# Adding the four components of a quaternion read by two VectorE sums instead of sixteen TensorE products

## The chip, the cores and the metric

One core of a Trainium2 chip runs the whole program once. The metric is the device time in microseconds (us); several executions are timed and their median is compared. Another execution is profiled; its span runs from its first to its last instruction. Below, PE is TensorE, DVE VectorE, ACT ScalarE, POOL GpSimd and SP the queue that issues DMAs.

## The reference, cut to what matters

Four layers follow each other on x of 4 x 1024 x 128: a time-mixing layer, a top-1 expert layer, a quaternion memory layer and a top-4 expert layer. The change is in the third:

```python
keys   = unit quaternions of (xn @ Wk.T + bk)       # 32 quaternions of 4 channels
values = (xn @ Wv.T + bv)
bound  = quat_mul(values, keys)
memory = jnp.cumsum(bound, axis=1)                  # over the tokens of a sequence
retrieved = quat_mul(memory, quat_conj(keys))       # the read
retrieved = retrieved / sqrt(position)
x = x + (layernorm(retrieved) * ln_g + ln_b) @ Wo.T + bo
```

Each output channel of a `quat_mul` is a sum of four products of a component of one factor with a signed component of the other.

## The kernel before, in words

All 4096 tokens stay in SBUF as `x_tok`. The memory layer is `memory_and_top4`. It takes 8 tiles of 512 tokens, each in 4 groups `s` of 128 tokens (a token per partition, 128 channels in the free dimension). The function `weave` writes out by hand what each engine issues: for tile `i` a `body` of 16 steps, and in each step first `tail(i-1)`, then `main(i)`, `ahead(i+1)` and `norm(i+2)`. So four tiles are under way, and each engine takes its instructions in this order. Behind the 8 bodies come `units`, the top-4 expert layer, 17 units a tile; the tail of tile 7 runs in its first ones, and its routing for tile 0 (`route`, `look`) runs in the bodies of tiles 6 and 7.

What a body does, by step, with the lines that the text speaks of:

- `ahead`: PE makes keys (`c_k`, L1453 and L1455, step 0) and values (`c_v`, step 4). ACT copies the keys in four signed orders (`key`, L1854 and L1860). DVE makes 1/length (L1625 a `tensor_reduce` over 4 adjacent elements, L1628, L1631) and divides the values by it (L1636, L1638).
- `main` step 0: products of key and value into `bound`, [128, s, 4 components, 128]: DVE s = 0 and 1 (L1647), POOL s = 2 and 3 (L1973).
- steps 1, 3, 5, 7: PE adds the four components and sums over the tokens in one go, with the triangular matrix `upto` as the moving operand (L1478), and adds the sum carried from the group before (L1483); ACT copies each result to `memory` (L1873).
- steps 8, 9: DVE divides `memory` by the key's length (L1653, and L1658 for s = 2 and 3 as `memory_n`).
- step 10: products for the read, into `read`: DVE s = 0, 1 (L1664), POOL s = 2, 3 (L1979).
- step 12: DVE makes the real part `real` (L1670, one for s = 0, 1 and one for s = 2, 3).
- steps 12 to 15: PE adds the four components of each group with the identity (L1494), sixteen products a tile, into the bank `bank_r`.
- `tail` steps 0 to 4: DVE makes `got` = 2 real - sum (L1678), its mean and variance (L1683, L1689), and, after POOL's power (L1985, L1989), the shift (L1693). Steps 6, 7: ACT normalises (L1881). Step 8: PE transposes (L1505), ACT L1888; step 11: PE multiplies with Wo (`c_o`); step 13: DVE adds the residual (L1698), which POOL had put ready at step 4 of `main` (`kept`, L1966).
- `norm`: statistics of the tile two ahead (DVE L1606, L1613, L1618; POOL L1957), ACT `xn` (L1839), and at step 12 PE transposes it (L1449) and ACT copies it (`xt`, L1846).

The lines around the change that a sentence can't say:

```python
for m in range(QC):                                     # L1493, PE, QC = 4
    mm = pe.matmul(bank_r[:, s * P:(s + 1) * P], ident, read[:, s, m, :], start=(m == 0), stop=(m == QC - 1))
...
dve.wait_ge(read_out, i + 1)                            # L1676, DVE, in front of got
```

An fp32 product of this shape leaves two records in the trace, so the 128 products of L1494 stand there as 256.

Of the kernel before, what the change touches and what calls it, by code (L numbers as in the profile page):

```python
# [9 lines left out]
ALU = mybir.AluOpType  # L10
ACT = mybir.ActivationFunctionType
AXIS = mybir.AxisListType
# [6 lines left out]
P = 128  # L19
BATCH, SEQ = 4, 1024  # L20
TOKENS = BATCH * SEQ
SUB = 4
# [52 lines left out]
def need(engine, semaphore, value):  # L75

    if not isinstance(value, int) or value > 0:
        engine.wait_ge(semaphore, value)
# [1026 lines left out]
QUATS, QC = P // 4, 4  # L1105
# [93 lines left out]
def memory_and_top4(nc, x_tok, consts, weights, out_dram, moe):  # L1199
# [3 lines left out]
    with ExitStack() as ctx:  # L1203
# [6 lines left out]
        def sem(name):  # L1210
            return nc.alloc_semaphore("c_" + name)
# [4 lines left out]
        ident = consts[:, C_AT["ident"][0]:C_AT["ident"][1]]  # L1216
# [47 lines left out]
        bound_dve, bound_pool = sem("bound_dve"), sem("bound_pool")  # L1264
        memory_out, memory_ready, memoryn_ready = sem("memory_out"), sem("memory_ready"), sem("memoryn_ready")
        read_dve, read_pool = sem("read_dve"), sem("read_pool")
        read_out, real_ready, got_ready = sem("read_out"), sem("real_ready"), sem("got_ready")
        stats2_ready, moments2_ready, var2_ready = sem("stats2_ready"), sem("moments2_ready"), sem("var2_ready")
        rstd2_ready, shift2_ready, normed_ready = sem("rstd2_ready"), sem("shift2_ready"), sem("normed_ready")
        normedt_out, normedt_ready, wo_out, x_ready = sem("normedt_out"), sem("normedt_ready"), sem("wo_out"), sem("x_ready")  # L1270
# [133 lines left out]
        with nc.Block() as block:  # L1404
# [38 lines left out]
            def _(pe):  # L1443
# [24 lines left out]
                def main(i, h, step):  # L1468
                    if step in (1, 3, 5, 7):
                        s = step // 2  # L1470
                        if s < 2:
                            pe.wait_ge(bound_dve, 2 * i + s + 1)
                        else:
                            pe.wait_ge(bound_pool, 2 * i + s - 1)
                        need(pe, memory_ready, SUB * i + s - 1)
                        carried = h or s
                        for m in range(QC):
                            mm = pe.matmul(bank_m[s % 2][:, 0:P], w("upto"), bound[:, s, m, :],  # L1478
                                           start=(m == 0), stop=(m == QC - 1 and not carried))
                        if carried:  # L1480
                            pe.wait_ge(memory_ready, SUB * i + s)
                            before = memory[:, h, s - 1, :] if s else memory[:, 1 - h, SUB - 1, :]
                            mm = pe.matmul(bank_m[s % 2][:, 0:P], w("last"), before, start=False, stop=True)  # L1483
                        mm.then_inc(memory_out, 1)
                    if step >= 12:
                        s = step - 12
                        if s == 0:
                            need(pe, got_ready, i)
                        if s < 2:
                            pe.wait_ge(read_dve, 2 * i + s + 1)  # L1490
                        else:
                            pe.wait_ge(read_pool, 2 * i + s - 1)
                        for m in range(QC):  # L1493
                            mm = pe.matmul(bank_r[:, s * P:(s + 1) * P], ident, read[:, s, m, :],  # L1494
                                           start=(m == 0), stop=(m == QC - 1))
                        if s == SUB - 1:
                            mm.then_inc(read_out, 1)

                def tail(i, h, step):
                    if step == 8:  # L1500
# [100 lines left out]
            def _(dve):  # L1601
# [39 lines left out]
                def main(i, h, step):  # L1641
                    if step == 0:
                        dve.wait_ge(valuen_ready, 2 * (i + 1))
                        dve.wait_ge(key_ready, i + 1)
                        need(dve, memory_out, SUB * i)
                        for s in (0, 1):
                            dve.tensor_tensor(in_quats(bound[:, s, :, :]), in_quats(key[:, h, s, :, :]),  # L1647
                                              spread_component(early_value[:, s, :]), ALU.mult).then_inc(bound_dve, 1)
                    if step == 8:
                        dve.wait_ge(memory_ready, SUB * (i + 1) - 2)  # L1650
                        dve.wait_ge(valuen_ready, min(2 * i + 3, 2 * TILES) if isinstance(i, int) else 2 * i + 3)
                        need(dve, real_ready, 2 * i)
                        dve.tensor_tensor(by_quat(early_n), by_quat(memory[:, h, 0:2, :]), per_quat(rnorm[:, h, 0:2 * QUATS]),  # L1653
                                          ALU.mult).then_inc(memoryn_ready, 1)
                    if step == 9:
                        dve.wait_ge(memory_ready, SUB * (i + 1))
                        need(dve, read_pool, 2 * i)
                        dve.tensor_tensor(by_quat(memory_n[:, :, :]), by_quat(memory[:, h, 2:4, :]), per_quat(rnorm[:, h, 2 * QUATS:]),  # L1658
                                          ALU.mult).then_inc(memoryn_ready, 1)
                    if step == 10:  # L1660
                        dve.wait_ge(memoryn_ready, 2 * (i + 1))
                        need(dve, read_out, i)
                        for s in (0, 1):
                            dve.tensor_tensor(in_quats(read[:, s, :, :]), in_quats(key[:, h, s, :, :]),  # L1664
                                              spread_component(early_n[:, s, :]), ALU.mult).then_inc(read_dve, 1)
                    if step == 12:
                        need(dve, got_ready, i)
                        for first, part in ((0, early_n), (2, memory_n[:, :, :])):
                            k0 = key[:, h, first:first + 2, 0, 0:P:QC]
                            dve.tensor_tensor(components(real[:, first:first + 2, :]), components(part),  # L1670
                                              k0.unsqueeze(3).broadcast_to([P, 2, QUATS, QC]), ALU.mult).then_inc(real_ready, 1)

                def tail(i, h, step):
                    if step == 0:
                        dve.wait_ge(real_ready, 2 * (i + 1))
                        dve.wait_ge(read_out, i + 1)  # L1676
                        need(dve, normed_ready, i)
                        dve.scalar_tensor_tensor(got[:, :, :].rearrange("p s c -> p (s c)"), real[:, :, :].rearrange("p s c -> p (s c)"),  # L1678
                                                 2.0, bank_r[:, :], ALU.mult, ALU.subtract).then_inc(got_ready, 1)
                    if step == 1:  # L1680
                        dve.wait_ge(got_ready, i + 1)
                        for s in range(SUB):
# [267 lines left out]
            def _(pool):  # L1950
# [11 lines left out]
                def main(i, h, step):  # L1962
# [11 lines left out]
                                               spread_component(value_n[:, s - 2, :]), ALU.mult).then_inc(bound_pool, 1)  # L1974
                    if step == 10:
                        pool.wait_ge(memoryn_ready, 2 * (i + 1))
                        need(pool, read_out, i)
                        for s in (2, 3):
                            pool.tensor_tensor(in_quats(read[:, s, :, :]), in_quats(key[:, h, s, :, :]),  # L1979
                                               spread_component(memory_n[:, s - 2, :]), ALU.mult).then_inc(read_pool, 1)  # L1980
# [134 lines left out]
```

## Time and profile before

| what | us |
|---|---|
| median of 3 runs | 950.02 (945.75 to 951.28) |
| the profiled execution, its own time | 945.13 |
| its span | 943.3 |
| its memory layer, first `got` to last | 491.4 to 598.9 |
| mean granted TensorE clock | 0.905 of 2.4 GHz |

A row of a timeline gives the start in us from the span's start, the duration in us, the engine, the line, the operation, what it writes and reads, and in brackets how long the engine had been idle before it and which instruction ended that. "x8" means eight merged instructions, whose duration is then that from the first start to the last end. "issue" is idle time that the view could give to no other engine.

### The profile page before, as it was taken

What the parts mean: (1) busy time and instruction counts of PE and PEld (TensorE: products, weight loads), DVE (VectorE), ACT (ScalarE), POOL (GpSimd) and SP (SyncE); (2) the same over time, 40 slices, a digit from 0 to 9 for tenths busy, and PEclk for the clock granted to TensorE, in tenths of its full rate; (3) what the DMA queues carried; (4) which work ended last, traced back from release to release, by engine and by line L of the source; (5) the groups of instructions that cost most, each with busy time, mean ns of one, the idle gap of its engine ahead of it and who ended that gap; (6) DMA issues with size and microseconds to landing.
All of it is one profiled execution on the core that took longest, in us unless ns stands there. A gap on an engine that the chain in (4) does not pass through costs nothing.

```text
span 943.3 us, 14234 instructions
## 1 busy us (share of the span) xinstructions
PE 789.7 (84%) x3827; PEld 563.7 (60%) x3828; DVE 653.4 (69%) x1483; ACT 429.4 (46%) x861; POOL 465.2 (49%) x424
## 2 busy tenths in 40 slices
PE   5888888996495599992289999899999999999997
PEld 2344444442395366661278888668686776868685
DVE  3899999998474133336458777686877868686864
ACT  3344445541121132233246555466565656657453
POOL 3465556664047133336136555355565555555564
PEclk9999999997555699996579999999999999999999
DMA  5000000000394111112000000537191745638090
GB/s 170 0 1 2 0 1 0 0 1 0 52 384 151 35 48 48 45 42 101 0 1 1 2 1 1 114 68 161 36 190 39 155 86 109 131 63 176 20 189 12
DMA packets 35662, 62.15 MB, mean 66 GB/s; under 512 B 3360, under 2 KB 15136, under 8 KB 34832
## 3 DMA queue, kind: packets, MB, share of 16 engines
q1 hardware_dynamic: 33328, 56.75, 25.5%
q0 software_dynamic: 2272, 4.67, 1.5%
q8 instruction: 27, 0.44, 0.2%
q14 instruction: 35, 0.29, 0.1%
HBM read 53.13 MB, written 8.28 MB: 65 GB/s over the span
## 4 chain that ended last, share of the span: by engine, by line
PE 24%; issue 11%; POOL 10%; DVE 3%; ACT 2%; DMA 1%; POOLq 0%; SPq 0%; ACTq 0%; DVEq 0%
POOL d_hid_lo L2006 5%; PE c_m L1513 2%; PE c_m L1515 2%; PE c_m L1514 2%; PE c_o L1564 1%; PE c_r L1564 1%; PE c_k L1513 1%; POOL c_bound L1973 1%; POOL c_read L1979 1%; PE c_k L1514 1%; PE c_k L1515 1%; PE c_v L1513 1%; PE c_o L1562 1%; PE c_o L1561 1%; PE c_v L1515 1%
## 5 line engine op out<-in xcount | busy, mean ns | idle before, releaser
L2006 POOL TENSOR_TENSOR d_hid_lo<-c_bound,d_hid_hi 128x512 fp32r<-128x512 f32 x136 | 176.1, 1295 | 156.1 <-ACT d_hid_hi L1936 155.8
L580 POOL TENSOR_TENSOR a_rs<-a_r,a_state 128x512 f32<-128x512 f32 x64 | 75.4, 1184 | 79.8 <-DVE a_state L432 74.1
L1936 ACT ACTIVATE d_hid_hi<-c_bound 128x512 fp32r<-128x512 f32 x136 | 85.2, 626 | 46.2 <-DVE c_bound L1804 45.6
L432 DVE TENSOR_TENSOR_SCAN a_state<-a_decay,a_state,a_vb 128x512 f32<-128x512 f32 x64 | 81.4, 1272 | 0.0
L1016 DVE TENSOR_TENSOR b_hidden<-b_h,b_b 128x512 f32<-128x512 f32 x39 | 27.0, 692 | 78.0 <-PE b_h L836 78.0
L1098 POOL DMA_INDIRECT results<-b_y_row,b_result_row x39 | 37.1, 953 | 86.3 <-DVE b_y_row L1022 86.3
L1795 DVE TENSOR_TENSOR c_m<-c_bound,c_m 128x512 f32<-128x512 f32 x64 | 44.2, 691 | 26.5 <-PE c_m L1515 20.5
L1795 DVE TENSOR_TENSOR c_v<-c_bound,c_v 128x512 f32<-128x512 f32 x64 | 44.2, 691 | 23.9 <-PE c_v L1515 18.7
L1513 PE MATMUL c_m<-d_x_hi,d_hi 128*128 128x512 f32 x136 | 55.8, 411 | 1.9 <-DVE c_bound L1804 1.9
L850 PEld LDWEIGHTS b_y<-b_w,b_hidden_t 128*128 128x128 f32 x312 | 39.1, 194 | 25.3 <-issue 25.2
L1515 PE MATMUL c_m<-d_x_hi,d_lo 128*128 128x512 f32 x136 | 53.9, 396 | 0.0
L1514 PE MATMUL c_m<-d_x_lo,d_hi 128*128 128x512 f32 x136 | 53.8, 395 | 0.0
L836 PE MATMUL b_h<-b_w,b_xin_t 128*128 x78 | 45.6, 668 | 7.1 <-issue 5.8
L1926 ACT ACTIVATE c_bound<-c_k 128x512 f32<-128x512 f32 x60 | 35.7, 595 | 34.4 <-PE c_k L1515 33.9
L1926 ACT ACTIVATE c_bound<-c_m 128x512 f32<-128x512 f32 x60 | 35.7, 595 | 34.3 <-PE c_m L1515 33.9
L570 POOL TENSOR_TENSOR a_xf<-a_lerp,a_xt 128x512 f32<-128x512 f32 x40 | 43.3, 1091 | 10.3 <-DVE a_lerp L395 10.0
L416 DVE TENSOR_TENSOR a_vb<-a_k,a_vb 128x512 f32<-128x512 f32 x64 | 43.2, 687 | 3.8 <-PE a_vb L304 3.8
L303 PE MATMUL a_vb<-a_v_hi,a_spread 128*128 128x512 f32 x64 | 44.5, 695 | 1.1 <-DVE a_state L432 1.1
L850 PE MATMUL b_y<-b_w,b_hidden_t 128*128 x312 | 44.3, 286 | 0.8 <-ACT b_hidden_t L1078 0.8
L1092 POOL DMA_INDIRECT rows_in<-b_rows,b_index x32 | 30.9, 965 | 26.7 <-DVE b_index L956 17.6
L1804 DVE TENSOR_TENSOR c_bound<-c_v,d_w_wide 128x512 f32<-128x512 f32 x56 | 38.7, 691 | 6.9 <-DMA d_w_wide<-pair_weights 4.5
L1075 ACT ACTIVATE b_xin_t<-b_x 128x128 f32<-128x128 f32 x38 | 10.6, 278 | 68.6 <-PE b_x L831 68.6
(299 smaller groups left out, 2184.0 us busy)
## 6 DMA issues: line engine op xcount, KB each, us to landing
d_w_wide<-pair_weights SPq DMA_DIRECT2D x64, 512.0 KB, 11.8
b_w<-in_w SPq DMA_DIRECT2D x2, 2048.0 KB, 15.5
d_raw<-in_moe SPq DMA_DIRECT2D x3, 1088.0 KB, 30.6
b_xin<-rows_in SPq DMA_DIRECT2D x39, 64.5 KB, 1.8
b_b<-in_b SPq DMA_DIRECT2D x1, 2048.0 KB, 21.9
b_rows<-results SPq DMA_DIRECT2D x4, 512.0 KB, 5.1
out<-c_read SPq DMA_DIRECT2D x8, 256.0 KB, 2.5
a_weights<-in_mixing SPq DMA_DIRECT2D x1, 901.0 KB, 6.5
```

The source lines that it names most:

```text
L303: pe.matmul(vb[n][:, :], row, v_hi[:, h, :], start=True, stop=False)
L432: dve.tensor_tensor_scan(state[:, j, seq_cols(h, 1)], decay[:, h, :], vb[j % 3][:, :], first, ALU.mult, ALU.add).then_inc(scan_ready, 1)
L580: pool.tensor_tensor(rs[:, j, :], rr[:, h, :], state[:, j, seq_cols(h, 0)], ALU.mult).then_inc(rs_ready, 1)
L836: pe.matmul(bank_h[h][:, :], xin_t[:, h, :], w1[:, bass.ds(e * D_FF, D_FF)], start=True, stop=True).then_inc(h_out, 1)
L850: mm = pe.matmul(bank_y[h][:, 0:P], hidden_t[:, h, f * P:(f + 1) * P], w2[:, bass.ds(e * D_FF + f * P, P)], start=(f == 0), stop=(f == FF_ ...
L1513: pe.matmul(out, weights_hi, moving_hi, start=start, stop=False)
L1514: pe.matmul(out, weights_hi, moving_lo, start=False, stop=False)
L1515: return pe.matmul(out, weights_lo, moving_hi, start=False, stop=stop)
L1795: dve.tensor_tensor(bank_3[r][:, :], silu[:, r, :], bank_3[r][:, :], ALU.mult).then_inc(product_ready, 1)
L1926: act.activation(silu[:, r, :], bank_1[r][:, :], ACT.Silu).then_inc(silu_ready, 1)
L1936: act.activation(hid_hi[:, r, :], hidden[:, r, :], ACT.Copy).then_inc(hi_ready, 1)
L2006: pool.tensor_tensor(hid_lo[:, r, :], hidden[:, r, :], hid_hi[:, r, :].bitcast(F32), ALU.subtract).then_inc(lo_ready, 1)
```

## The change

PE's sixteen products with the identity, and PE's waits around them, go. DVE gets two `tensor_reduce` instructions a tile, at steps 13 and 15 of `main`, each over two groups: 1024 elements in, 256 out, the summed axis being the components, which lie 128 elements (512 bytes) apart. `got` then reads both its operands from SBUF, where it read one from PSUM. The semaphore `read_out` (PE) is replaced by `summed` (DVE).

```diff
@@ PE, main
-                    if step >= 12:
-                        s = step - 12
-                        if s == 0:
-                            need(pe, got_ready, i)
-                        if s < 2:
-                            pe.wait_ge(read_dve, 2 * i + s + 1)
-                        else:
-                            pe.wait_ge(read_pool, 2 * i + s - 1)
-                        for m in range(QC):
-                            mm = pe.matmul(bank_r[:, s * P:(s + 1) * P], ident, read[:, s, m, :],
-                                           start=(m == 0), stop=(m == QC - 1))
-                        if s == SUB - 1:
-                            mm.then_inc(read_out, 1)
@@ DVE, main
                     if step == 10:
                         dve.wait_ge(memoryn_ready, 2 * (i + 1))
-                        need(dve, read_out, i)
...
+                    if step in (13, 15):
+                        if step == 13:
+                            dve.wait_ge(read_dve, 2 * (i + 1))
+                            need(dve, normed_ready, i)
+                        else:
+                            dve.wait_ge(read_pool, 2 * (i + 1))
+                        pair = slice(0, 2) if step == 13 else slice(2, 4)
+                        dve.tensor_reduce(got[:, pair, :], read[:, pair, :, :].rearrange("p s m c -> p s c m"), AXIS.X,
+                                          ALU.add).then_inc(summed, 1)
@@ DVE, tail
                     if step == 0:
                         dve.wait_ge(real_ready, 2 * (i + 1))
-                        dve.wait_ge(read_out, i + 1)
-                        need(dve, normed_ready, i)
-                        dve.scalar_tensor_tensor(got[:, :, :].rearrange("p s c -> p (s c)"), real[:, :, :].rearrange("p s c -> p (s c)"),
-                                                 2.0, bank_r[:, :], ALU.mult, ALU.subtract).then_inc(got_ready, 1)
+                        dve.wait_ge(summed, 2 * (i + 1))
+                        dve.scalar_tensor_tensor(got[:, :, :], real[:, :, :], 2.0, got[:, :, :],
+                                                 ALU.mult, ALU.subtract).then_inc(got_ready, 1)
@@ POOL, main
                     if step == 10:
                         pool.wait_ge(memoryn_ready, 2 * (i + 1))
-                        need(pool, read_out, i)
+                        need(pool, summed, 2 * i)
```

## Rows read from the trace of the kernel before

**Rows 1.** Stretches `got` to `got`: length, busy PE PEld DVE ACT POOL (count), clock, DMA

```profile
521.24:536.17 14.93, 13.94 (x108) 12.42 (x108) 11.89 (x33) 8.53 (x23) 8.81 (x9) 1.00 0.00 0
536.17:553.05 16.88, 15.62 (x106) 13.91 (x106) 12.02 (x33) 8.52 (x23) 8.81 (x9) 0.90 0.01 1
...
567.98:582.47 14.49, 13.34 (x104) 11.95 (x105) 11.68 (x33) 7.82 (x22) 8.82 (x9) 1.00 0.01 2
```

**Rows 2.** Timeline of DVE, the body between two `got`

```profile
521.24 0.69 DVE L1678 SCALAR_TENSOR_TENSOR c_got<-c_real,c_r 128x512 f32<-128x512 f32 x1 [1.88 <-issue]
...
530.39 0.42 DVE L1658 TENSOR_TENSOR c_memory_n<-c_memory,c_rnorm 128x256 f32<-128x256 f32 x1
...
532.38 1.30 DVE L1670 TENSOR_TENSOR c_real<-c_memory_n,c_key 128x256 f32<-128x256 f32 x1
533.61 0.68 DVE L1698 TENSOR_TENSOR x_tok<-c_o,c_kept 128x512 f32<-128x512 f32 x1
536.17 0.69 DVE L1678 SCALAR_TENSOR_TENSOR c_got<-c_real,c_r 128x512 f32<-128x512 f32 x1 [1.89 <-issue]
```

**Rows 3.** Timeline of PE, the same body

```profile
522.59 1.16 PE L1478 MATMUL c_m<-c_bound,memory_weights 128*128 128x128 f32 x8
...
528.44 0.39 PE L1483 MATMUL c_m<-c_memory,memory_weights 128*128 128x128 f32 x2
...
532.80 0.60 PE L1449 MATMUL c_x<-shape_consts,c_xn 128*128 128x128 f32 x4
533.23 2.84 PE L1494 MATMUL c_r<-c_read,shape_consts 128*128 128x128 f32 x24
...
536.44 1.16 PE L1455 MATMUL c_k<-memory_weights,c_xt 128*128 128x128 f32 x8
```

**Rows 4.** Timelines of ACT and POOL, the same body

```profile
529.34 0.27 ACT L1873 ACTIVATE c_memory<-c_m 128x128 f32<-128x128 f32 x1
...
530.51 1.65 ACT L1839 ACTIVATE c_xn<-x_tok,c_shift,c_rstd 128x128 f32<-128x128 f32 x4
533.43 0.60 ACT L1846 ACTIVATE c_xt<-c_x 128x512 f32<-128x512 f32 x1 [1.27 <-PE c_x L1449]
```

```profile
533.36 2.68 POOL L1973 TENSOR_TENSOR c_bound<-c_key,c_value_n 128x512 f32<-128x512 f32 x2
```

**Rows 5.** Groups of instructions by form: count, busy us, mean ns of one, idle before

```profile
L1494 PE MATMUL c_r<-c_read,shape_consts 128*128 128x128 f32 x256 | 32.1, 280 | 2.1 <-DVE c_read L1664 2.1
```

```profile
L1625 DVE TENSOR_REDUCE c_norm<-c_square 128x128 f32<-128x512 f32 x8 | 5.3, 666 | 14.1 <-ACT c_square L1856 13.9 <-issue 0.2
```

**Rows 6.** Lines L960 (reads 32 bytes apart), L946 (adjacent): duration ns min/median/max

```profile
L960 DVE TENSOR_REDUCE b_here<-b_chosen x8: 171/206/208, 264.1 to 294.4; 128x8 f32<-128x32 f32 x8
```

```profile
L946 DVE TENSOR_REDUCE b_position<-b_own_place x8: 180/180/186, 268.3 to 296.9; 128x4 f32<-128x32 f32 x8
```

**Rows 7.** Timeline of PE: gaps, and the instructions behind them

```profile
58.05 1.82 PE L244 MATMUL a_front<-a_xa,a_weights 128*128 128x512 f32 x2 [2.58 <-DVE a_xa L387]
...
487.00 1.16 PE L1494 MATMUL c_r<-c_read,shape_consts 128*128 128x128 f32 x8 [1.55 <-DVE c_read L1664]
...
547.78 1.92 PE L1494 MATMUL c_r<-c_read,shape_consts 128*128 128x128 f32 x8
...
608.03 0.80 PE L1513 MATMUL c_v<-d_x_hi,d_hi 128*128 128x512 f32 x1 [2.93 <-DVE c_bound L1804]
```

**Rows 8.** Busy time by stretch behind three gaps of PE, columns as in rows 1

```profile
58.00:61.00 3.00, 2.95 (x5) 1.64 (x6) 3.00 (x7) 0.60 (x1) 0.53 (x2) 0.56 0.00 0
...
111.00:114.00 3.00, 2.45 (x6) 1.06 (x6) 3.00 (x8) 0.79 (x2) 0.56 (x2) 1.00 0.00 0
```

```profile
608.00:611.40 3.40, 3.37 (x11) 2.75 (x11) 3.37 (x12) 2.29 (x4) 1.77 (x2) 0.51 1.07 210
```

**Rows 9.** Timeline of DVE, the last body and the first unit

```profile
587.60 0.29 DVE L1737 TENSOR_REDUCE d_minus_max<-c_d 128x4 f32<-128x128 f32 x1 [0.82 <-PE c_d L1515]
...
607.28 0.69 DVE L1804 TENSOR_TENSOR c_bound<-c_v,d_w_wide 128x512 f32<-128x512 f32 x1 [4.45 <-DMA d_w_wide<-pair_weights]
```

More of the change, by code:

```diff
@@ L1266, in memory_and_top4 @@
         read_dve, read_pool = sem("read_dve"), sem("read_pool")
-        read_out, real_ready, got_ready = sem("read_out"), sem("real_ready"), sem("got_ready")
+        summed, real_ready, got_ready = sem("summed"), sem("real_ready"), sem("got_ready")
         stats2_ready, moments2_ready, var2_ready = sem("stats2_ready"), sem("moments2_ready"), sem("var2_ready")
```

## The prediction, on record before the changed kernel ran

> **What bounds the kernel now.** I read the stretches from one `got` (L1678) to the next first, since each is one tile of the memory layer. There are seven. Four last 14.92 to 14.94 us, of which one is shown; one 16.88, the only one at a mean clock below full; then 14.49, and a last one that holds the first routing [rows 1]. In the shown stretch PE is busy 13.94 us and DVE 12.42: two engines close to the length, so the timeline has to say which waits for which. DVE waits 1.88 or 1.89 us in front of `got` [rows 2]. The view calls it issue, but PE's last products of L1494 end at 533.23 + 2.84 = 536.07 and `got` starts at 536.17 [rows 2, 3]: DVE waits for the work that the change removes. Behind `got` comes DVE's half of `bound`, and PE's next c_m waits for that (it starts at 522.59, 1.35 after `got` at 521.24) [rows 2, 3]. So the loop is closed through both engines. But between the two waits for `got` DVE has almost nothing free: from 521.24 to the end of L1698 at 533.61 + 0.68 = 534.29 is 13.05 us, with one larger wait in it, for POOL's power.
>
> **What goes.** L1494 holds PE 32.1 us in 8 tiles, 4.0 a tile [rows 5]. What the time gets back is not that but DVE's wait, at most 1.89 us a tile, because DVE's 13.05 us stay. PE's waits at these steps go too. The waits of DVE and POOL at step 10 are met by DVE's order (the sums of a tile stand long before its successor's reads), and the wait for `normed` moves to step 13, long after ACT has normalised. No DMA moves.
>
> **What comes.** Two sums of 1024 elements. The nearest row is L1625: 512 elements in 0.666 us; L946 takes 0.180 for 32 [rows 5, 6]. The slope is 0.486 / 480 = 1.01 ns an element, so 1024 take 0.666 + 0.52 = 1.18 us. Neighbouring DVE instructions overlap by 0.08 (533.61 starts before 532.38 + 1.30 = 533.68 [rows 2]), so each adds 1.10. The low bound is 1.05, a nanosecond an element with nothing fixed left. The high bound comes from the distance between summed elements. L1625's are adjacent, the new ones 512 bytes apart. L960 sums elements 32 bytes apart: 206 ns in the median, but 171 in its shortest, against 180 at L946 with adjacent ones [rows 6]. Taken at its worst that is 26 / 32 = 0.81 ns more an element, 0.83 us more a sum, 2.0 us each. I take 1.18, because the shortest of the strided ones shows no penalty at all, and the others start right on the heels of a tiny conversion, whose end their record may include.
>
> The Trainium skill speaks against this change here: "Advanced Engine Details and Errata", section SBUF Cachelines, says that accesses that each hit another 16-byte line pay a penalty. By that rule the sums would be dear, and the rival below says how dear; the 171 ns speak against it, the 206 for it.
>
> `got` now reads two operands from SBUF. What that can cost is shown by L1670's second instruction: 1.30 us for 256 elements while POOL's multiplications of the read ran, and it ended 0.32 behind POOL's switch from L1979 to L1973 at 533.36 [rows 2, 4]. It had waited for POOL. POOL's `bound` products end at 533.36 + 2.68 = 536.04 [rows 4]. The new `got` comes after that (next paragraph), so I take nothing; at worst it starts when POOL ends, which costs nothing either while the sums end later.
>
> **The sum, a tile at full clock.** The first sum starts at 534.21, the second ends at 534.21 + 2 x 1.10 + 0.08 = 536.49, `got` starts 0.04 later, at 536.53. Before it was 536.17 [rows 2]. So a tile loses 0.36 us: 2.24 of sums against 1.89 of wait. Over the bodies: four with 14.93 give +1.44. The one of 16.88 becomes 15.29, -1.59, since its length came from PE running at half clock, which DVE would no longer wait for. The one of 14.49 has a larger wait and comes out at +0.05. The one before the first `got` is a draw. Tile 7's sums and `got` run about 1 us later, and are covered by the 4.45 us in which DVE waits for the weights of the first unit [rows 9]. Together -0.1 us: at full clock the change is worth nothing.
>
> **PE's clock.** PE now gets a hole. Its transposes of `xn` can start when ACT is done at 530.51 + 1.65 = 532.16 [rows 4] and end 0.6 later; ACT's copy takes 0.60 and the keys 1.53 (from 536.07 to 536.44 + 1.16), until about 535.0 [rows 3, 4]. The next c_m can start only 1.35 behind `got`, at 537.88. That is a hole of over 2.8 us a tile where PE was without one. What such holes do here is in the trace. In the time-mixing layer PE waits some 2.6 us (2.58 at 58.05) or more in front of L244 in each of seven tiles; behind six of these waits the clock fell to 1.2 GHz, as at 58 to 61 (mean 0.56), and behind one, at 111 to 114, it stayed at 2.4 [rows 7, 8]. After 2.93 us at 608.03 it fell too (0.51) [rows 7, 8]. After 1.55 us at 487.00 it stayed [rows 7]. At half clock eight records of L1494 take 1.92 us and not 1.16 [rows 7].
>
> What it costs: the low stretch at 608.0 to 611.4 lasts 3.4 us [rows 8], in which PE does half the work and falls 1.7 us behind. The c_m ends at 528.44 + 0.39 = 528.83; ACT's copy of it starts at 529.34 and ends 529.61, and DVE wants it at 530.39 [rows 2, 3, 4]. The slack is 0.44 + 0.78 = 1.2 us. So one stretch costs 0.5 us; two in a row, where the first begins inside the hole, 3.4 - 1.2 = 2.2. I take 0.9, nearer to the single one. And not every tile pays: a PE that is late also has a shorter hole the next time. I take four of the six tiles, +3.6. Then the last body. Body 6 has no keys to make, so the hole there is from 10.9 + 0.6 behind `got` to 14.5 + 1.35, some 4.4 us. Behind it stand c_m and the logits, and DVE already waits 0.82 for those at L1737 [rows 9], the chain that leads over the weights and their DMA to 607.28. No slack: +1.7. (To +3.4 with two.)
>
> **The sum.** -0.1 + 3.6 + 1.7 = +5.2 us. The profiled execution took 945.13 by its own time (span 943.3); the median of the runs is 950.02, 4.9 above it, so I put the difference on the median: 955.2.
>
> **Rivals.**
> - *The clock stays up* (or its loss falls into slack). For it: one of seven holes passed without a fall, DVE is the bound, and PE then has 4 us to spare. Against: the other six. Time: 950.02 - 0.1 = 949.9, no change that can be measured. It decides at a hole below about 2 us.
> - *The strided sums cost 2.0 us each*, the rule of "Advanced Engine Details and Errata" as a mechanism of this kernel: DVE as the plain bound, 17 us a tile. 7 bodies x 2 x 0.83 = 11.6 more on top: 966.8. Against it the 171 ns.
> - *Not slower, faster*: PE sets the pace of the loop and DVE has hidden room, so that removing PE's work lets DVE's chain close up, where it waits for POOL's power and where L1670 waits for POOL. If the order of POOL and DVE shifts so that L1670 runs before POOL's products (0.42 in place of 1.30 [rows 2]), a tile gains 0.9 - 0.36 = 0.5 us, in 7 bodies 3.8, and the slow stretch of 16.88 stays away: about 945. It decides if L1670's second instruction falls below 1 us. Against: both wait for the same `memory_n`, and DVE's reads stand first.
> - *The edit does something else than it says*, say the sum is split into more instructions: not visible in the diff, covered by the second rival.
>
> **How the numbers follow.** About 0.5%, 4.75 us, is what a measurement of this kernel can tell from no change. Forecast case, time lost through the clock: 0.54, its own range 951 to 961. Clock stays up: 0.22. Dear strides: 0.12. Faster: 0.08. The rest, 0.04, beyond all. The range of 8 in 10 runs from 946 (the clock stays up, with the spread of 5 us between runs of before) to 966, near dear strides. Slower by over 0.5% (above 954.8): 0.32 of the forecast case, dear strides 0.12, and the rest 0.04: 0.48. Within: the forecast case's lower 0.22 and the 0.22 in which the clock stays up: 0.44. Faster: 0.08.
>
> **What would show it.** No L1494 on PE; sixteen `tensor_reduce` of 1024 elements on DVE at 1.15 to 1.25 us (2.0 under the stride rival); `got` to `got` 15.3 us where the clock is full; `got` with no idle time before it; holes of 2 to 3 us in front of c_m (L1478), and mean clocks of 0.8 to 0.9 in the stretches behind; DVE idle in front of L1658 in those, which it isn't now; in the last body L1737 waiting over 2 us. DVE's busy time rises by 2.2 a tile, 18 us. I am wrong if the stretches sit at 15.3 with full clock everywhere (then no change), if they are under 14.9 (then DVE had room that I didn't see), or over 16.5 at full clock (then the sums are dear).

## The result, and the profile after

| what | before | after |
|---|---|---|
| median of 4 runs, us | 950.65 (945.75 to 952.4) | 973.24 (972.16 to 974.08) |
| ratio | | 1.026 [1.023, 1.0291] |
| profiled execution, its own time | 945.13 | 972.16 |
| its span | 943.3 | 970.3 |
| mean granted clock | 0.905 | 0.881 |

The kernel became slower: the ratio on record is 1.026 (the quotient of the two medians is 1.024), 22.6 us in the medians and 27.0 in the profiled executions. The forecast was 955.2, the range ended at 966. The lines of the changed kernel are numbered anew: `got` L1672, the sums L1665, `bound` L1634, `memory_n` L1645, the read L1650, shift L1687.

The stretches from one `got` to the next, columns as in [rows 1]:

```profile
494.97:513.03 18.06, 12.78 (x75) 10.86 (x75) 15.79 (x36) 8.36 (x23) 8.80 (x9) 0.84 0.00 0
513.03:530.39 17.36, 12.08 (x73) 10.23 (x73) 15.65 (x36) 8.36 (x23) 8.81 (x9) 0.90 0.01 1
530.39:547.83 17.44, 12.16 (x75) 10.31 (x75) 15.64 (x35) 8.36 (x23) 8.81 (x9) 0.90 0.00 0
547.83:566.40 18.57, 13.29 (x73) 11.15 (x73) 15.64 (x36) 8.36 (x23) 8.81 (x9) 0.79 0.01 1
...
601.85:622.45 20.60, 16.55 (x100) 14.43 (x101) 17.07 (x52) 10.13 (x24) 6.15 (x7) 0.72 0.02 6
```

The reader sees three things. DVE's busy time rose from 12.0 to 15.7 us a tile (3.7, where the forecast had 2.2). No stretch has the full clock any more. And in the first six the length exceeds DVE's busy time by 1.7 to 2.9 us, where 1.3 are left at full clock (filled_hole, below), so DVE is not all of it. The group of the sums gives their price; its shortest, 1866 ns, is nearly as dear as its median:

```profile
L1665 DVE TENSOR_REDUCE c_got<-c_read x16: 1866/1918/1991, 491.1 to 620.4; 128x256 f32<-128x1024 f32 x16
```

DVE and PE in the third stretch:

```profile
530.39 0.69 DVE L1672 SCALAR_TENSOR_TENSOR c_got<-c_real,c_got 128x512 f32<-128x512 f32 x1
531.00 1.28 DVE L1634 TENSOR_TENSOR c_bound<-c_key,c_v 128x512 f32<-128x512 f32 x2
...
534.98 1.22 DVE L1687 SCALAR_TENSOR_TENSOR c_shift<-c_moments,c_rstd 128x4 f32<-128x4 f32 x1 [0.83 <-POOL c_rstd L1983]
...
540.17 0.42 DVE L1645 TENSOR_TENSOR c_memory_n<-c_memory,c_rnorm 128x256 f32<-128x256 f32 x1 [0.55 <-ACT c_memory L1867]
...
542.17 1.29 DVE L1656 TENSOR_TENSOR c_real<-c_memory_n,c_key 128x256 f32<-128x256 f32 x1
543.38 0.68 DVE L1692 TENSOR_TENSOR x_tok<-c_o,c_kept 128x512 f32<-128x512 f32 x1
543.99 3.74 DVE L1665 TENSOR_REDUCE c_got<-c_read 128x256 f32<-128x1024 f32 x2
547.83 0.69 DVE L1672 SCALAR_TENSOR_TENSOR c_got<-c_real,c_got 128x512 f32<-128x512 f32 x1
```

```profile
531.73 2.08 PE L1478 MATMUL c_m<-c_bound,memory_weights 128*128 128x128 f32 x8 [3.71 <-DVE c_bound L1634]
...
544.30 1.16 PE L1455 MATMUL c_k<-memory_weights,c_xt 128*128 128x128 f32 x8
549.17 2.07 PE L1478 MATMUL c_m<-c_bound,memory_weights 128*128 128x128 f32 x8 [3.71 <-DVE c_bound L1634]
```

`got` has no idle time before it, where it had 1.89 [rows 2]; the sums take its place and 1.9 us more. PE, which had no hole there, waits 3.71 us, and the first c_m behind the hole takes 2.08 and not 1.16 [rows 3]: the clock has fallen. DVE then waits 0.55 for ACT's copy of that late product, a wait that was absent in the stretch shown of before; in the six bodies between the first `got` and the seventh it is 0.46 to 1.68.

**Where the 27.0 us are**, from start times in the two timelines:

| part | before | after | more |
|---|---|---|---|
| to the stage's first PE instruction (L1449) | 461.07 | 463.19 | 2.1 |
| from there to the first `got` | 30.3 | 31.8 | 1.5 |
| first `got` to last | 107.5 | 127.5 | 20.0 |
| last `got` to the first product with `w_wide` | 8.4 | 5.9 | -2.5 |
| from there to the first copy of `y` | 46.9 | 48.9 | 2.0 |
| the seven tiles of units behind it | 283.2 | 286.9 | 3.6 |
| the end | 5.8 | 6.1 | 0.3 |

The first line is not the change's: in twelve other profiled executions it ranges from 457.5 to 464.2, with no relation to the edit. Below, "the stage" is the second to fourth line together: 146.2 us before, 165.1 after. The 146.2 hold the one body of 16.88 us [rows 1], 2 us longer than its neighbours.

### The profile page after: what moved, and what is told of

Same layout as the page of the kernel before. It is cut to its first block, busy times and chain, and to the rows that moved or that the text cites. A ratio compares the mean times of both kernels' runs of the same rounds, so it can differ in the third digit from the quotient of the medians.

```text
span 970.3 us, 13731 instructions
## 1 busy us (share of the span) xinstructions
PE 781.1 (80%) x3571; PEld 549.6 (57%) x3572; DVE 685.9 (71%) x1499; ACT 427.8 (44%) x861; POOL 462.9 (48%) x424
## 4 chain that ended last, share of the span: by engine, by line
PE 27%; issue 9%; DVE 8%; POOL 6%; ACT 3%; POOLq 0%; DVEq 0%; ACTq 0%
POOL d_hid_lo L2000 5%; PE c_m L1478 4%; DVE c_got L1665 3%; PE c_m L1500 2%; PE c_m L1502 2%; PE c_m L1501 2%; PE c_o L1551 1%; PE c_r L1551 1%; PE c_k L1500 1%; PE c_k L1501 1%; PE c_k L1502 1%; PE c_o L1549 1%; PE c_o L1548 1%; PE c_v L1502 1%; PE c_v L1500 1%
## 5 line engine op out<-in xcount | busy, mean ns | idle before, releaser
L1478 PE MATMUL c_m<-c_bound,memory_weights 128*128 128x128 f32 x256 | 46.9, 347 | 27.2 <-DVE c_bound L1634 27.2
L1478 PEld LDWEIGHTS c_m<-c_bound,memory_weights 128*128 128x128 f32 x256 | 43.3, 257 | 28.7 <-DVE c_bound L1634 28.7
## 6 DMA issues: line engine op xcount, KB each, us to landing
d_w_wide<-pair_weights SPq DMA_DIRECT2D x64, 512.0 KB, 11.6
```

## The experiments

Theories for the 19 us of the stage: **S**, the sums cost 1.92 us and not 1.18, and DVE is the bound; **C**, the clock falls in PE's hole; **O**, the new body brings DVE's and POOL's instructions together in a worse order. Each run is timed against the kernel before on its own chip. The table has what all of them gave. The columns are the ratio of the times as it stands on record, with its 95% interval (it can differ by 0.2% from the quotient of the medians), then, from one profiled execution each, the stage, a typical body (the middle ones), and the clock in it.

| run | ratio | stage | body | clock |
|---|---|---|---|---|
| before | 1 | 146.2 | 14.93 | 1.00 |
| after_again | 1.0253 [1.0216, 1.0291] | 165.1 | 17.4 to 18.5 | 0.79 to 0.90 |
| adjacent | 1.0213 [1.0175, 1.025] | 159.1 | 16.9 to 17.2 | 0.80 |
| filled_hole | 1.0259 [1.0217, 1.0301] | 165.2 | 16.9 | 1.00 |
| drop_only | 0.9905 [0.9868, 0.9943] | 136.5 | 13.4 to 14.0 | 0.88 to 1.00 |
| add_only | 1.0173 [1.0135, 1.0212] | 158.4 | 16.65 | 1.00 |
| layout | 1.0218 [1.0181, 1.0255] | 159.1 | 16.8 to 17.2 | 0.80 |
| ordered_strided | 1.0183 [1.0153, 1.0213] | 159.7 | 16.8 to 17.5 | 0.84 to 0.90 |
| ordered_layout | 1.0133 [1.0106, 1.016] | 155.7 | 15.6 to 16.9 | 0.80 to 0.89 |
| ordered_layout_filled | 1.0157 [1.0141, 1.0172] | 159.4 | 15.3 to 15.6 | 1.00 |
| before_ordered | 0.9993 [0.998, 1.0005] | 144.7 | 14.6 to 14.8 | 1.00 |
| hybrid_plain | 0.9988 [0.9974, 1.0002] | 141.2 | 14.4 | 1.00 |
| hybrid | 0.9915 [0.9899, 0.993] | 139.6 | 13.5 | 1.00 |

**adjacent: the same number of elements, summed over four neighbours.** The output is made of other numbers.

```diff
-dve.tensor_reduce(got[:, pair, :], read[:, pair, :, :].rearrange("p s m c -> p s c m"), AXIS.X,
+dve.tensor_reduce(got[:, pair, :], read[:, pair, :, :].rearrange("p s m (q c) -> p s (m q) c", c=QC), AXIS.X,
```

> The changed kernel, but each sum runs over four adjacent channels of one component in place of the four components 512 bytes apart (same element counts, so the output is other numbers). If the distance between summed elements makes the sums dear: 1.18 us each where the changed kernel has 1.92, got to got 15.3 to 16 us, and a time of 958 to 964, 10 or more below the changed kernel. If size or shape (1024 in, 256 out) or POOL beside it makes them dear: still 1.9 us and 973. If the clock alone makes the loss: sums may shorten, but the time stays above 968.

The group of the sums in this run, then its PE and a DVE instruction in one body:

```profile
L1665 DVE TENSOR_REDUCE c_got<-c_read x16: 1201/1202/1208, 484.9 to 608.2; 128x256 f32<-128x1024 f32 x16
```

```profile
521.73 2.08 PE L1478 MATMUL c_m<-c_bound,memory_weights 128*128 128x128 f32 x8 [2.31 <-DVE c_bound L1634]
523.61 0.63 PE L1483 MATMUL c_m<-c_memory,memory_weights 128*128 128x128 f32 x2
524.03 1.91 PE L1478 MATMUL c_m<-c_bound,memory_weights 128*128 128x128 f32 x8
...
531.39 0.42 DVE L1645 TENSOR_TENSOR c_memory_n<-c_memory,c_rnorm 128x256 f32<-128x256 f32 x1 [1.74 <-ACT c_memory L1867]
```

The stride costs 1918 - 1202 = 716 ns a sum, 0.70 ns an element. But this run is also the forecast's own world, sums at 1.2 us, and it is still 2.1% slower than before. Behind a hole of 2.3 us the clock is down for two groups of c_m, in every body but the first, and DVE then waits 1.5 to 1.8 us for the late product. These bodies take 16.9 to 17.2 us with DVE busy for 14.2. So the sums' price came as the first theory had it, and its body of 15.3 to 16 us did not.

**filled_hole: after, with sixteen products with the identity behind the keys, which nobody reads.**

```diff
 project(bank_k, "bk", "wk", xt).then_inc(k_out, 1)
+for s in range(SUB):
+    for m in range(QC):
+        pe.matmul(bank_r[:, s * P:(s + 1) * P], ident, w("upto"), start=(m == 0), stop=(m == QC - 1))
```

> The changed kernel with sixteen products of the identity put behind the keys on PE, into a bank that nobody reads, so that PE's hole is filled with as much work as was taken out. If the fallen clock costs what the waits in front of L1645 (7.5 us) and L1731 (2.4) and the first unit show: full clock in the memory layer, got to got 17.0 in every body, 962 to 966. If the sums alone make the loss: 971 to 973, no change.

Its stretches:

```profile
529.18:546.05 16.87, 14.29 (x110) 12.39 (x109) 15.62 (x35) 8.53 (x23) 8.82 (x9) 1.00 0.00 1
546.05:562.93 16.88, 14.14 (x108) 12.24 (x107) 15.63 (x35) 8.53 (x23) 8.81 (x9) 1.00 0.01 1
```

With PE filled the clock stays at 2.4 GHz in six bodies (mean 0.99 in the sixth). The middle four take 16.87 to 16.90 us, near the 17.0 of the first theory, and before's timeline says why: the sums begin 534.21 - 521.24 = 12.97 behind `got` as the forecast had it, and take 3.84 until the next `got` (543.99 to 547.83 above), together 16.81. So at full clock S alone is the whole body. C is 127.5 - 122.1 = 5.4 us from first to last `got`. The time gained nothing that the ratio shows (1.0259), because the same products run at half clock where the stage starts and nothing covers them; the first `got` comes 37.4 us behind the stage's first instruction, not 31.8. PE in that start, where the view puts the fillers under c_r:

```profile
460.24 2.07 PE L1455 MATMUL c_k<-memory_weights,c_xt 128*128 128x128 f32 x8
462.11 5.44 PE L1466 MATMUL c_r<-memory_weights,shape_consts 128*128 128x128 f32 x32
...
477.01 4.85 PE L1466 MATMUL c_r<-memory_weights,shape_consts 128*128 128x128 f32 x32
```

**drop_only and add_only: each half of the change alone.** The first leaves the sum of the components out altogether (`got` = 2 real - real). The second keeps PE's products and lets DVE also make the sums of tiles 0 to 6, into a buffer that nobody reads.

```diff
 # drop_only, against after
-dve.tensor_reduce(got[:, pair, :], read[:, pair, :, :].rearrange("p s m c -> p s c m"), AXIS.X,
-                  ALU.add).then_inc(summed, 1)
+dve.sem_inc(summed, 2)
-dve.scalar_tensor_tensor(got[:, :, :], real[:, :, :], 2.0, got[:, :, :],
+dve.scalar_tensor_tensor(got[:, :, :], real[:, :, :], 2.0, real[:, :, :],
```

> The removal alone: no products of L1494 and no sums (the sum is left out, got is made from real alone). DVE as the bound: got to got 13.2 to 14.9 at full clock (13.05 of DVE's own, and got, with two SBUF operands, may wait for POOL's products of bound until 14.8). With the clock falling as in the changed kernel one or two bodies of it are given back: 943 to 952. If PE had set the pace alone: got to got 11, 922.

> The addition alone: the kernel before, with the two strided sums of tiles 0 to 6 made on DVE beside PE's products and read by nobody. If the sums on DVE are the larger loss: got to got 17.0 (13.05 + 3.74 and the seam) at full clock, since PE has no hole: 950 + 7 x 2.1 = 964 or somewhat over. If the clock were the larger loss: the sums would still fill the 1.9 us of wait and little more, 955 to 958.

A body of each, drop_only first:

```profile
513.09:526.53 13.44, 10.74 (x77) 8.84 (x77) 12.29 (x35) 8.52 (x23) 9.27 (x10) 1.00 0.00 0
```

```profile
524.56:541.20 16.64, 14.02 (x107) 12.42 (x107) 15.49 (x36) 8.52 (x24) 8.83 (x9) 1.00 0.00 0
```

Even for nothing in return, PE's sixteen products are worth 1.5 us a body (less in the two of 13.98 and 13.93 us, in which the clock fell behind a hole of only 0.87) and 1% of the time: that is the ceiling of the change. The sums alone cost 1.7 us a body and 1.7%, at full clock, though PE's holes in front of c_m are 1.6 us in these bodies. In drop_only `got` starts while POOL still multiplies, and takes this:

```profile
513.09 1.16 DVE L1667 SCALAR_TENSOR_TENSOR c_got<-c_real 128x512 f32<-128x512 f32 x1
```

That is 1.16 and not the 0.69 of [rows 2]. In the changed kernel the sums push `got` behind POOL and it takes 0.69, as the forecast said.

**after_again and layout.** The first repeats the changed kernel beside the others. The second writes `read` with the four components adjacent, so that the sums are cheap and are still those of the components:

```diff
-read = sb("read", [P, SUB, QC, P])
+read = sb("read", [P, SUB, P, QC])
```

> The changed kernel once more, so that it stands on the same chip as the three below. Sums of 1.92 us, got to got 17.3 to 18.6, some 2.3 to 2.7% above the kernel before.

> The changed kernel with read laid out so that the four components of a channel are adjacent: the same sums and the reference's output, read by DVE at distance 4 bytes in place of 512; the products of DVE and POOL (L1650, L1973) now write elements 16 bytes apart. If distance between elements costs in reads alone: sums 1.20 us, products 0.68 and 1.27 as before, got to got 17.0 with the clock falling as in the run with adjacent sums, some 10 us under the changed kernel. If writes at a distance cost as much as reads: the products take 0.36 more each, DVE's four writes of 512 a tile give back 0.7 of the 1.4 saved, and POOL's take 1.6 us and are on the path to the second sum.

Who pays for the turned layout, DVE's read products, POOL's and the sums:

```profile
L1976 POOL TENSOR_TENSOR c_read<-c_key,c_memory_n 128x512 f32<-128x512 f32 x16 | 20.3, 1291 | 23.2 <-DVE c_memory_n L1648 23.2
L1668 DVE TENSOR_REDUCE c_got<-c_read 128x256 f32<-128x1024 f32 x16 | 18.6, 1204 | 0.0
L1653 DVE TENSOR_TENSOR c_read<-c_key,c_v 128x512 f32<-128x512 f32 x16 | 16.5, 1116 | 0.3
```

Beside them the same products of adjacent, which write as the kernel before does:

```profile
L1973 POOL TENSOR_TENSOR c_read<-c_key,c_memory_n 128x512 f32<-128x512 f32 x16 | 20.0, 1270 | 23.9 <-DVE c_memory_n L1645 23.9
L1650 DVE TENSOR_TENSOR c_read<-c_key,c_v 128x512 f32<-128x512 f32 x16 | 10.3, 683 | 0.3
```

Writes 16 bytes apart cost DVE 433 ns a product and POOL some 20. Yet layout and adjacent have the same stage, 159.1, and DVE is busy for the same 14.2 to 14.3 us a body. The reason is the second real part, which takes 0.63 us here and 1.29 in adjacent:

```profile
537.56 0.63 DVE L1659 TENSOR_TENSOR c_real<-c_memory_n,c_key 128x256 f32<-128x256 f32 x1
```

In both runs it ends 0.3 us behind POOL's read products (534.67 against 534.39 in adjacent, 538.19 against 537.92 here). So the dearer writes used time in which the real part would have been held up beside POOL. Against after_again layout is 0.35% lower and adjacent 0.40%, which the intervals don't separate from nothing; the stage is 6.0 us shorter in each.

**ordered_strided and ordered_layout: theory O.** POOL's `kept` waits for DVE's shift and POOL's `bound` for `got`; the second real part moves behind the sums. On the changed kernel, and on layout.

```diff
 # POOL, main, steps 4 and 0
+need(pool, shift2_ready, i)
+need(pool, got_ready, i)
 # DVE, main
     if step == 12:
         real_part(h, 0, early_n)
...
+    if step == 15:
+        real_part(h, 2, memory_n[:, :, :])
```

> The changed kernel, sums still 512 bytes apart, with three moves that keep DVE's instructions with two SBUF operands away from POOL's: kept (L1960) waits for the shift, POOL's products of bound wait for got, and the second real part comes behind the sums. If DVE sets the pace through waits for POOL: L1687 falls from 1.22 to 0.16 us, the second L1656 from 1.29 to 0.41, together 1.9 a tile, got to got from 17.3 to 15.4 to 15.8, and 10 to 14 us less than the changed kernel. If DVE's order is not the bound (clock or ACT): no change of over 3 us.

> Both together. DVE's own chain is then 13.05 - 1.06 - 0.88 + 2.3 = 13.4 us, and PE's hole shrinks to about 1 us, at which the clock held before. If the reading is right: got to got 13.4 to 13.8 at full clock, 8 to 10 us under the kernel before (0.990 of it). If the clock still falls in every body: 15 and more, no gain over the kernel before. If strided writes are dear: 14.5, about 3 under.

DVE in ordered_strided:

```profile
527.16 0.41 DVE L1630 TENSOR_TENSOR c_real<-c_memory_n,c_key 128x256 f32<-128x256 f32 x1
...
532.20 0.16 DVE L1691 SCALAR_TENSOR_TENSOR c_shift<-c_moments,c_rstd 128x4 f32<-128x4 f32 x1 [0.83 <-POOL c_rstd L1989]
```

The shift falls from 1.22 to 0.16 us and the real part from 1.29 to 0.41. That takes 15.64 - 14.19 = 1.4 us of DVE's busy time from a body and not the 1.9 of both, since `c_norm_max` (L1615), now beside POOL's `kept`, takes 0.73 us in place of 0.20. The time falls by 0.7%, 7 us, and the bodies stay at 16.8 to 17.5 us where the first theory had 15.4 to 15.8: DVE waits instead for the products that the low clock delays. On layout it is 0.85%, and its bodies of 15.6 to 16.9 us are those of the second theory, the clock falling in each. Of that the stage gave 5.4 us in the first and 3.4 in the second; some 2.5 more are in the first unit tile, which the section on the prediction comes back to.

**ordered_layout_filled**, the same with the fillers of filled_hole.

> The ordered layout run (960.33, got to got 15.6 to 16.9 us) with 16 products with the identity that nobody reads, behind the keys on PE, as in the filled hole run. Theory that the fallen clock still costs it 1 to 2 us a body: the clock stays full in the bodies, got to got 14.2 to 14.9 us, 950 to 956 us, ratio 1.002 to 1.008. Rival that DVE's own chain is all of it: got to got as without the filling, ratio 1.012 to 1.016.

```profile
544.32:559.65 15.33, 13.76 (x107) 12.10 (x106) 13.42 (x35) 8.38 (x23) 8.73 (x9) 1.00 0.01 2
559.65:575.22 15.57, 14.00 (x109) 12.34 (x109) 13.44 (x36) 8.37 (x23) 8.74 (x9) 1.00 0.00 1
```

Neither theory held: the time is the rival's (1.0157), but the clock is full and the bodies shrank, to 15.3 to 15.6 and not to 14.2 to 14.9. There PE is busy for 13.8 to 14.0 us, its c_m starts at the end of the fillers with no idle time (562.36, when DVE's first `bound` product, begun at 560.26, is long there), and DVE waits 0.78 and 1.00 us for `memory`. And from stage start to first `got` went 35.7 us, against 28.8 in ordered_layout. The fillers cost 6.9 us in the start, and from first to last `got` the full clock gave back only 2.9 (119.0 to 116.1).

**before_ordered**, the control: POOL's two waits in the kernel before.

> The kernel before with the two waits that the ordered runs add on POOL (the kept addition behind shift2, the bound products behind got). Control for the order moves. Theory that PE bounds the body of the kernel before, so that DVE's operations slowed by POOL's cost nothing there: got to got 14.9 us as before, ratio 0.997 to 1.003. Rival that the order is worth the same 0.7% there as in the changed kernel: got to got 14.0 to 14.4 us, ratio 0.991 to 0.995. If POOL's bound products come late for PE the ratio is above 1.003.

`got` waits longer there, the bodies are 0.1 to 0.3 us shorter, and from first to last `got` nothing is left of it (107.1 us against 107.5):

```profile
517.83 0.69 DVE L1678 SCALAR_TENSOR_TENSOR c_got<-c_real,c_r 128x512 f32<-128x512 f32 x1 [2.23 <-issue]
```

What DVE saves it spends waiting for PE (2.23 against 1.89 [rows 2]). The order is worth nothing as long as PE ends last, and 0.7% once DVE does.

**hybrid and hybrid_plain.** PE sums the components of the groups whose products DVE writes (8 products a tile). DVE sums those of the other two groups in one adjacent reduction, since POOL writes them 16 bytes apart for some 20 ns. `got` becomes two instructions, one of which reads PSUM. hybrid has POOL's two waits, hybrid_plain doesn't; both real parts stay at step 12 in both, so of the three moves that the expectation names hybrid has two.

```diff
 # PE, main, steps 12 and 13 (s = 0, 1)
+    for m in range(QC):
+        mm = pe.matmul(bank_r[:, s * P:(s + 1) * P], ident, read[:, s, m, :], start=(m == 0), stop=(m == QC - 1))
 # POOL, step 10 (s = 2, 3); read_late is read[:, 2:4] seen as "p s (c m) -> p s c m"
-    pool.tensor_tensor(in_quats(read[:, s, :, :]), in_quats(key[:, h, s, :, :]),
+    pool.tensor_tensor(in_quats_late(s), in_quats(key[:, h, s, :, :]),
 # DVE, step 15, and tail step 0
+    dve.tensor_reduce(got[:, 2:4, :], read_late, AXIS.X, ALU.add).then_inc(summed, 1)
+    dve.scalar_tensor_tensor(got[:, 0:2, :], real[:, 0:2, :], 2.0,
+                             bank_r[:, 0:2 * P].rearrange("p (s c) -> p s c", s=2), ALU.mult, ALU.subtract)
+    dve.scalar_tensor_tensor(got[:, 2:4, :], real[:, 2:4, :], 2.0, got[:, 2:4, :], ALU.mult, ALU.subtract)
```

> Components of subtiles 0 and 1 (read products of DVE) are summed by PE again (8 products, the rows of the kernel before), those of subtiles 2 and 3 (read products of POOL) by one DVE reduction over adjacent elements, which POOL writes for free (1290 against 1275 ns in the layout run); plus the three order moves of the ordered runs. Theory that the price of the sums (1.9 us strided) and the 3.7 us hole of PE are what costs: DVE gives up one reduction (-1.2 us against the ordered layout run, -0.43 x 2 for its dense writes) and adds one more instruction for got (+0.6); the hole shrinks to about 1 us, the clock stays up in the bodies, got to got 13.3 to 14.2 us against 14.94 before, 930 to 941 us, ratio 0.985 to 0.995. Rival that any part of the sums on DVE makes DVE the bound and the clock falls with it: got to got 15.5 or more, ratio 1.005 to 1.015. Rival that POOL's read products (2.6 us after the memory) set the end of both: got to got near 14.9, ratio 0.998 to 1.003.

> The hybrid run without the two waits on POOL (nothing of the order is changed against the kernel before; both real parts stand where they stood). It tells how much of the hybrid's 0.9915 is the split of the sums and how much the order. Theory that DVE bounds the hybrid's body (13.5 us), so that its shift2 of some 1.0 us beside POOL's kept addition (157 ns in the ordered runs) and its got beside POOL's bound products are paid in full: got to got 14.2 to 15.0 us, ratio 0.996 to 1.000. Rival that the split alone carries it: got to got 13.5 to 13.8 us, ratio 0.990 to 0.993. Rival that DVE's longer body opens PE's hole over 2 us and the clock falls in it: got to got 15 us or more, ratio above 1.002.

A stretch of hybrid, then its DVE and PE:

```profile
530.20:543.68 13.48, 12.22 (x92) 10.63 (x93) 12.38 (x36) 8.49 (x23) 8.73 (x9) 1.00 0.01 2
```

```profile
534.84 0.16 DVE L1706 SCALAR_TENSOR_TENSOR c_shift<-c_moments,c_rstd 128x4 f32<-128x4 f32 x1 [0.83 <-POOL c_rstd L2004]
...
542.56 1.21 DVE L1681 TENSOR_REDUCE c_got<-c_read 128x256 f32<-128x1024 f32 x1
543.68 0.41 DVE L1687 SCALAR_TENSOR_TENSOR c_got<-c_real,c_r 128x256 f32<-128x256 f32 x1
544.01 0.41 DVE L1691 SCALAR_TENSOR_TENSOR c_got<-c_real,c_got 128x256 f32<-128x256 f32 x1
```

```profile
531.59 2.05 PE L1484 MATMUL c_m<-c_bound,memory_weights 128*128 128x128 f32 x16 [0.38 <-DVE c_bound L1655]
```

The hole in front of c_m is 0.38 us, the clock stays full, and the body is 13.48, as the first theory had it. hybrid takes 937.49 us against 944.73 of before on its chip. That is a small gain, 0.85% by the ratio, but the interval [0.9899, 0.993] leaves 1 out, and with it hybrid is faster than both kernels. The split without the order is at 14.4 us a body and 0.9988, no change, as its first theory had it; its shift takes this:

```profile
534.60 1.23 DVE L1706 SCALAR_TENSOR_TENSOR c_shift<-c_moments,c_rstd 128x4 f32<-128x4 f32 x1 [0.83 <-POOL c_rstd L2002]
```

So the order, worth nothing in before, is worth 0.9 us a body here, and by the ratios the two parts win only together. The profiles show only a part of that: from first to last `got` hybrid is 4.6 us shorter than hybrid_plain, but 1.1 us longer ahead of it and 1.9 behind it, 1.6 in the stage. Another 2.6 us are in the first unit tile (46.8 against 49.4), and no run ties those to the order.

## Why the prediction was wrong

- **The bound and the ceiling: right.** DVE waited for L1494, at most 1.89 us a body; drop_only gave 1.49 back (14.93 to 13.44), the rest went into a dearer `got`.
- **"I take 1.18": a term of the sum that was mis-sized.** The group shows 1.92 us. My high bound from the 206 ns of L960 [rows 6], 2.0, was right, and trusting the shortest record, 171, was the error: their median stood at 206, and here even the shortest, 1.87 us, has nearly the full penalty. The rule of the Trainium skill's "Advanced Engine Details and Errata", SBUF Cachelines, holds: the trace agrees, with 1918 against 1202 ns. With 1.92 in its place the forecast's own working gives 14.93 + 0.36 + 2 x 0.74 = 16.8 us a body at full clock, and filled_hole shows 16.88.
- **"I take 0.9", "four of the six tiles": the step that failed on its own.** The mechanism was right, holes in front of c_m and a fallen clock behind them, but adjacent, whose sums cost what I took, is at 1.0213 and not at the forecast's 1.005. Its bodies last 16.9 to 17.2 us where I had 15.3 at full clock, and DVE's wait in front of L1645 says where they went: 1.5 to 1.8 us a body, in every one but the first. I weighed one hole of seven that the clock survived, and priced a single low stretch as the usual case; in adjacent two in a row (6.8 us) were usual, behind a hole of 2.3 us (I had reckoned with over 2.8). The rival's "decides at a hole below about 2 us" fits the steady bodies: the clock fell behind 2.03 us in ordered_layout and stayed behind 1.6 in add_only. But the hole in front of c_m doesn't settle it alone, since in drop_only the clock fell behind 0.87 in two bodies and not in the others; why there stays open.
- **Adding the two terms would have been wrong too.** S at full clock makes a body of 16.9 (filled_hole), C with the cheap sums one of 17.0 (adjacent), and both together 17.3 to 18.6 (after). From first to last `got` that is 14.6 us over before, 14.7 and 20.0. Each hides most of the other: time that DVE needs anyway covers late products, and waiting for late products covers dearer sums. That is why curing either moved the ratio by 0.5% or less. The rival of dear strides, 966.8, had added its 11.6 us to a small clock term.
- **The last body, +1.7: right in sum, in part by luck.** The wait that I named came (L1737 is L1731 here):

```profile
608.56 0.29 DVE L1731 TENSOR_REDUCE d_minus_max<-c_d 128x4 f32<-128x128 f32 x1 [2.42 <-PE c_d L1502]
```

It is 1.6 us longer than the 0.82 of before [rows 9]. The stretch grew by 4.2 us in all, the dearer sums among them, and 2.5 came back before the first product with `w_wide`.
- **The rivals.** Clock up: excluded by every body. Faster through a quicker real part: it took 1.29 us, as before. The sum was not split: sixteen instructions, as the diff says.

**The units behind the stage: not foreseen.** No step of mine reached them, and they took 5.6 us more. 3.6 are tiles of 43.2 us in place of 42.1, three in after and none in before. Within such a tile DVE and POOL race. The shift of the top-4 layer (L1717, in after L1711) reads two SBUF operands; in before it starts 0.01 us ahead of POOL, in after behind it:

```profile
749.23 0.14 DVE L1717 SCALAR_TENSOR_TENSOR d_shift<-d_moments,d_rstd 128x4 f32<-128x4 f32 x1
```

```profile
749.24 1.30 POOL L2006 TENSOR_TENSOR d_hid_lo<-c_bound,d_hid_hi 128x512 fp32r<-128x512 f32 x1 [0.97 <-ACT d_hid_hi L1936]
```

```profile
730.54 1.03 DVE L1711 SCALAR_TENSOR_TENSOR d_shift<-d_moments,d_rstd 128x4 f32<-128x4 f32 x1
```

```profile
730.26 1.29 POOL L2000 TENSOR_TENSOR d_hid_lo<-c_bound,d_hid_hi 128x512 fp32r<-128x512 f32 x1 [0.99 <-ACT d_hid_hi L1930]
```

In the tiles of 42.1 us the shift takes 0.14 or 0.15 us, in those of 43.2 it takes 0.95 to 1.18. In the one shown it is late because the four MAX8 just ahead of it (L1744) stand idle for 0.19 us in their midst, which the view gives to no engine. Three tiles of 43.2 us stand in the profile of every kernel whose DVE makes the sums of all four groups, one in each hybrid, and never in before, before_ordered or drop_only. The code of the units is the same in all. Why the sums decide that race for the whole next layer stays open; no run was made on it. The other 2.0 us, in the first unit tile, can't be laid to the change: that tile takes 46.4 to 46.9 or 48.9 to 49.8 us, drop_only, before_ordered and hybrid_plain have the longer one too, and filled_hole and the ordered runs with all sums on DVE the shorter. What decides it stays open.

## What to carry to other kernels

Work that moves to the engine that waits must cost it less than its wait (here 1.5 us a tile), and a stall that the move opens on TensorE is to be priced as a fallen clock in every turn of the loop; here holes of 2.0 us did it in one turn after the other, and holes of 1.6 us did not. Price a strided reduction from the median of the nearest strided row. Where two costs close the same loop from two engines, the body is near the longer of them and not the sum, so curing one shows little; split the work so that neither engine has a long hole, and only then look at the order. Work put in only to fill a hole also runs where nothing covers it, here in the start of the stage.

## What the runs showed of the hardware

- A DVE sum of 1024 fp32 elements takes 1.202 us over neighbours and 1.918 at 512 bytes, 0.70 ns more an element. The 26 ns for 32 elements of L960 [rows 6] are 0.81.
- The same product of 512 elements, written 16 bytes apart, takes 1116 ns and not 683 on DVE, and 1291 and not 1270 on POOL. Who writes a turned layout matters more than the layout.
- TensorE's clock fell to 1.2 GHz behind holes of 2.03 (ordered_layout), 2.31 (adjacent) and 3.71 us (after) in one body after the other, and stayed at 2.4 in the bodies with holes of 0.4 to 0.7 (hybrid), 0.4 to 0.8 (filled_hole), 1.2 (hybrid_plain) and 1.6 us (add_only) there. In drop_only, with 0.87, it fell in two bodies and stayed in the others.
- A DVE instruction with two SBUF operands on four elements a partition takes 0.14 to 0.16 us alone and 0.95 to 1.23 beside a POOL instruction on 512. In after the shift L1687 starts at 534.98 and ends at 536.20, right behind this one of POOL (534.91 + 1.26 = 536.17):

```profile
534.91 1.26 POOL L1960 TENSOR_TENSOR c_kept<-c_xn,x_tok 128x512 f32<-128x512 f32 x1
```

The Trainium skill's "SBUF — State Buffer", section "SBUF: two separate sides", says of GpSimd and of a DVE instruction with two SBUF inputs (against a GpSimd instruction that reads SBUF) that the one that starts first holds a shared port pair for its whole instruction and the other is blocked. The trace agrees, with the 0.03 us between the two ends, and in the units a start 0.01 us earlier was enough to escape it.
